# Cell states of a two-layer transformer block finished batch by batch beside the next batch's cells

## What is computed

```python
x = x + tanh(g_xattn[1]) * L1_xattn(layernorm(x), ctx, ctx)   # cells, 16 heads
x = x + tanh(g_ffn[1]) * L1_ffn(layernorm(x))
# in L1_xattn, for each batch and head:
C = (q @ k.T / sqrt(16)) * D            # D = exp(gates), lower triangle
h = (C / (max(|C.sum(-1)|, exp(-m)) + eps)) @ v
h = (h - h.mean(-1)) * rsqrt(h.var(-1) + eps) * ln_scale      # per head
# in L1_ffn, for each token:
inter = silu(q_act(x) @ q_w(w_gate).T) * (q_act(x) @ q_w(w_up).T)
y = q_act(inter) @ q_w(w_down).T        # q_act: blocks of 32, shared exponent, 3 fraction bits
```

## Time and profile before

| what | us |
|---|---|
| median of 3 runs (494.81 to 496.61) | 495.32 |
| the profiled execution, its own time | 496.37 |
| its span, first to last instruction | 494.6 |
| DVE busy in the span | 349.6 |
| PE busy, PE weight load busy | 381.1, 258.7 |
| ACT busy, POOL busy | 189.1, 152.8 |

### The profile page before, as it was taken

The page is one execution under the profiler, slowest core; times in us unless marked ns, Lnnn a source line. Parts: engine busy times, 40 slices in busy tenths (PEclk is TensorE's granted clock), DMA queues, the critical chain, the costliest instruction groups (busy, mean ns, idle before and its releaser), DMA issues.

```text
span 494.6 us, 6936 instructions
## 1 busy us (share of the span) xinstructions
PE 381.1 (77%) x2330; PEld 258.7 (52%) x2330; DVE 349.6 (71%) x857; ACT 189.1 (38%) x331; POOL 152.8 (31%) x147
## 2 busy tenths in 40 slices
PE   7899787799997697959767887979577478660745
PEld 3566454545556585848545555657353156440323
DVE  4586259257633989887976657577995976789895
ACT  4456424323313122603343545444004577640331
POOL 4029300028425445546325223233212020030240
PEclk9999997579998989979995999999697759966695
DMA  8900000003402203302986930907000670000001
GB/s 280 254 12 0 9 1 1 1 1 107 129 0 65 85 12 122 104 20 88 201 187 89 164 104 0 141 31 107 2 0 0 106 129 1 2 0 1 23 20 45
DMA packets 33714, 32.69 MB, mean 66 GB/s; under 512 B 3876, under 2 KB 32784, under 8 KB 33680
## 3 DMA queue, kind: packets, MB, share of 16 engines
q1 hardware_dynamic: 31088, 28.99, 26.4%
q0 software_dynamic: 992, 1.68, 1.2%
q10 hardware_dynamic: 1600, 1.57, 1.0%
HBM read 28.04 MB, written 4.19 MB: 65 GB/s over the span
## 4 chain that ended last, share of the span: by engine, by line
PE 49%; DVE 24%; issue 12%; ACT 6%; POOL 3%; DMA 3%; SPq 1%; DVEq 0%; ACTq 0%; POOLq 0%
PE bank L869 14%; PE bank L895 6%; PE bank L781 5%; PE bank L797 3%; PE bank L754 3%; PE bank L1005 2%; PE bank L969 2%; DVE mxraw L1610 2%; DVE mam L1452 2%; DVE tok L1262 2%; PE bank L765 1%; PE bank L917 1%; PE bank L954 1%; DVE probs L1537 1%; DMA qrep<-part_dram 1%
## 5 line engine op out<-in xcount | busy, mean ns | idle before, releaser
L895 PE MATMUL bank<-wexp,wT 128*128 128x256 f32 x192 | 53.9, 406 | 7.7 <-DVE x L1444 7.6
L869 PE MATMUL bank<-tok_r,probs_r 128*128 128x512 f32 x104 | 48.0, 462 | 11.6 <-DVE wT L1433 7.0
L1322 DVE TENSOR_SCALAR probs<-probs,hi 128x512 f32<-128x512 f32 x64 | 34.6, 592 | 28.8 <-ACT probs L1077 28.7
L663 POOL TENSOR_TENSOR wexp_r<-wexp,probs_r 128x1024 fp32r<-128x1024 f32 x13 | 31.2, 2403 | 60.3 <-ACT probs_r L1088 60.3
L1127 ACT ACTIVATE silu_sb<-bank 128x512 f32<-128x512 f32 x32 | 19.1, 597 | 77.1 <-PE bank L869 77.1
L1077 ACT ACTIVATE probs<-bank 128x1024 f32<-128x1024 f32 x32 | 32.2, 1025 | 41.1 <-PE bank L781 41.1
L591 POOL TENSOR_TENSOR mx_grid<-parts,bl 128x1024 bf16<-128x1024 fp8e4 x9 | 17.2, 1910 | 96.0 <-DVE parts L1613 96.0
L895 PEld LDWEIGHTS bank<-wexp,wT 128*128 128x128 f32 x192 | 37.1, 203 | 15.3 <-issue 10.5
L1537 DVE SCALAR_TENSOR_TENSOR probs<-bank,dexp 128x384 f32<-128x384 f32 x48 | 26.4, 554 | 24.0 <-PE bank L955 17.7
L869 PE MATMUL bank<-tok_r,wexp_r 128*128 128x512 f32 x104 | 42.7, 411 | 0.0
L781 PE MATMUL bank<-qrep,krep 32*128 32x256 f32 x256 | 35.8, 410 | 1.8 <-issue 1.0
(11 more groups left out here) (261 smaller groups left out, 895.9 us busy)
## 6 DMA issues: line engine op xcount, KB each, us to landing
wexp<-in_L_ffn_W SPq DMA_DIRECT2D x28, 256.0 KB, 4.1
krep<-part_dram SPq DMA_DIRECT2D x32, 128.0 KB, 6.6
qrep<-part_dram SPq DMA_DIRECT2D x32, 128.0 KB, 4.6
wexp<-in_L_ffn_Wg SPq DMA_DIRECT2D x14, 256.0 KB, 4.6
part_dram<-parts POOLq DMA_DIRECT2D x4, 384.0 KB, 3.0
part_dram<-parts SPq DMA_DIRECT2D x4, 384.0 KB, 3.3
x<-in_x ACTq DMA_DIRECT2D x2, 512.0 KB, 7.2
ctx<-in_ctx SPq DMA_DIRECT2D x2, 512.0 KB, 7.0
```

What stands on the lines that cost most here:

```text
L663: gp.tensor_tensor(low, raw, w_high[k % 2].bitcast(F32), ALU.subtract).then_inc(s["w_low_ready"], 1)
L869: mm = pe.matmul(bank[:, bk, :], lhs, rhs, start=(kk == 0 and q == 0), stop=(kk == KC - 1 and q == len(terms) - 1))
L895: mm = pe.matmul(bank[:, 2 + pair, D * t:D * t + D], hid[k % 2][m][:, col:col + P], wexp[:, k % WR, 2, m, :], start=(m == 0), stop=(m == 1))
L1322: ins = v.tensor_scalar(w, w, hi[:, 2 * b + kc:2 * b + kc + 1], EM50, ALU.min, ALU.max)
```

## The change

The cell groups run batch by batch: group g is now batch g//2 with heads g%2. So batch 0 is complete after group 1, batch 1 after group 3, batch 2 after group 5, batch 3 after group 7. The finish works on one batch, 2 tiles, 128x512, and there are four of them: batch 0's beside group 3, batch 1's in experts 14 and 15, batch 2's beside group 7, batch 3's behind the last group. GpSimd scales in place in tok and waits for the square in place of the centring. The quantiser of tok works on a batch too (512 columns, items 0, 1, 5 and 8 of now 12); the quantiser of tile 2 stands between scores 33 and 34, that of batch 2 behind score 63; q_turn of tile 1 stands in group 6. krep units 2 and 3 are loaded at groups 2 and 3. quantise(0) stands behind accumulate 31, not before accumulate 30. The functions of DVE, ACT, TensorE and GpSimd take the sizes from q_wide and ln_tiles; where the diff below leaves them out, nothing else changes in them.

```diff
-    def cells(g, first=0):
+    def cells(g, first=0, more=()):
...
-            units.append(u)
+            units.append(u + (more[j] if j < len(more) else []))
...
-    def finish(n):
-        return st("cell_in", n) + st("cell_mid", n) + st("cell_out", n) + st("ln_in", 6 + n) + st("ln_out", 6 + n)
+    def finish(b):
+
+        return [st("cell_in", b), st("cell_mid", b), st("cell_out", b), st("ln_in", 6 + b), st("ln_out", 6 + b)]
+
+    def beside_cells(b, last=[]):
+        f = finish(b)
+        return [f[0], [], f[1], [], f[2], [], f[3], f[4] + last]
 
     plan += expert(8, 5) + weave(expert(9, 6), prepare(0)[:2] + [[]] + prepare(0)[2:4]) + weave(expert(10, 7)[:6], prepare(0)[4:]) + expert(10, 7)[6:8] + st("turn_gates", 0)
-    plan += weave(expert(10, 7)[8:] + flat([expert(k, k - 3) for k in range(11, 14)]), flat([cells(g) for g in range(4)]) + cells_end(3))
-    plan += weave(expert(14, 11) + expert(15, 12), finish(0))
-    plan += st("out", 30, 31) + st("quantise", 0) + st("accumulate", 30, 31)
-
-
-
-    line = [(1, 0), (2, 1), (3, 2), (4, None), (5, 3), (6, 4), (7, 5), (8, 6), (9, 7)]
+    plan += weave(expert(10, 7)[8:] + flat([expert(k, k - 3) for k in range(11, 14)]),
+                  flat([cells(g, 0, beside_cells(0) if g == 3 else ()) for g in range(4)]) + cells_end(3))
+    plan += weave(expert(14, 11) + expert(15, 12), flat(finish(1)))
+    plan += st("out", 30, 31) + st("accumulate", 30, 31) + st("quantise", 0)
+
+
+    line = [(2, 0), (3, 1), (4, 2), (5, None), (6, 3), (7, 4), (8, None), (9, 5), (10, 6), (11, 7)]
...
-    plan += st("q_turn", 0) + ready[:2] + flat(stage_d(0)[:3]) + ready[2:] + flat(stage_d(0)[3:]) + st("turn_gates", 1)
+    plan += ready[:2] + st("q_turn", 0) + st("quantise", 1) + flat(stage_d(0)[:3]) + ready[2:] + st("q_turn", 1) + flat(stage_d(0)[3:]) + st("turn_gates", 1)
     plan += flat(stage_d(1) + stage_d(2)[:3])
-    plan += weave(flat([cells(g, 4) for g in range(4, 8)]), [[]] + stage_d(2)[3:]) + flat(cells_end(7))
-    plan += weave(finish(1), stage_d(3)[:3]) + flat(stage_d(3)[3:])
-    plan += flat(flat([stage_d(j) for j in range(4, len(line) + 4)]))
+    early = stage_d(3)
+    plan += flat(cells(4, 4, [[], stage_d(2)[3]])) + flat(cells(5, 4)) + flat(cells(6, 4, [[], early[0] + early[1] + early[2]]))
+    plan += flat(cells(7, 4, beside_cells(2, early[3])))
+    plan += flat(cells_end(7))
+    plan += weave(flat(finish(3)), stage_d(4) + stage_d(5))
+    plan += flat(flat([stage_d(j) for j in range(6, len(line) + 4)]))
...
-        hstat = arows[:, :, :].rearrange("p a t -> p (a t)")[:, 0:6 * NH * 64].rearrange("p (q n h) -> p q n h", q=6, n=NH)
+        hstat = arows[:, :, :].rearrange("p a t -> p (a t)")[:, 0:6 * B * 32].rearrange("p (q b h) -> p q b h", q=6, b=B)
+        hst = lambda q, b: hstat[:, q, b, :]
...
-        NQ = NT + NH
-        q_half = {0: 0, 4: 1}.get
-        q_tile = lambda k: k - 1 if k < 4 else k - 2
+        q_batch = {0: 0, 1: 1, 5: 2, 8: 3}.get
+        q_tile = {2: 0, 3: 1, 4: 2, 6: 3, 7: 4, 9: 5, 10: 6, 11: 7}.get
+        NQ = NT + B
+        q_wide = lambda k: 2 * D if q_tile(k) is None else NI
 
         def q_source(k):
 
-            if q_half(k) is None:
+            if q_tile(k) is not None:
                 return inter[:, q_tile(k) % 2, :]
-            return tok[:, TH * q_half(k):TH * q_half(k) + TH, :].rearrange("p t d -> p (t d)")
+            return tok[:, 2 * q_batch(k):2 * q_batch(k) + 2, :].rearrange("p t d -> p (t d)")
...
+        def cell_group(g):
+
+            return g // 4, g % 2, g // 2, (g // 2 % 2) * S, 2 * (g // 4) + g % 2
...
+        def ln_tiles(k):
+
+            return range(TH * (k % 2), TH * (k % 2) + TH) if k < 6 else range(2 * (k - 6), 2 * (k - 6) + 2)
+
+        def ln_stat(ap, k):
+            return ap[:, k, :] if k < 6 else ap[:, 6 + (k - 6) // 2, 2 * (k % 2):2 * (k % 2) + 2]
...
-                    sp.wait_ge(s["qk_done"], 16 * (u - 1))
+                    sp.wait_ge(s["qk_done"], 8 * (u + 1))
...
-                if g in (1, 3):
+                if g in (2, 3):
                     sp.wait_ge(s["qk_done"], 8 * (g + 1))
-                    u = (g + 3) // 2
-                    stack_load(sp, krep, u % 2, 1, u, K_TERM, s[f"k_stacked{u}"])
+                    stack_load(sp, krep, g % 2, 1, g, K_TERM, s[f"k_stacked{g}"])
...
-                gp.wait_ge(s["h_centred"], n + 1)
-                gp.tensor_tensor(pvs[:, :, :].rearrange("p a (u d) -> p (a u) d", d=D), tok[:, TH * n:TH * n + TH, :],
-                                 lsc[:, :].unsqueeze(1).broadcast_to([P, TH, D]), ALU.mult).then_inc(s["h_scaled"], 1)
+                gp.wait_ge(s["h_squared"], n + 1)
+                h = tok[:, 2 * n:2 * n + 2, :]
+                gp.tensor_tensor(h, h, lsc[:, :].unsqueeze(1).broadcast_to([P, 2, D]), ALU.mult).then_inc(s["h_scaled"], 1)
...
-                pe.wait_ge(s["xqt_copied"], i // TH + 1)
+                pe.wait_ge(s["xqt_copied"], i // 2 + 1)
...
-                act.activation(mt[:, :, :].rearrange("p a t -> p (a t)"), tok[:, TH * n:TH * n + TH, :].rearrange("p t d -> p (t d)"),
-                               ACT.Square).then_inc(s["h_squared"], 1)
+                act.activation(mt[:, n % 2, :], tok[:, 2 * n:2 * n + 2, :].rearrange("p t d -> p (t d)"), ACT.Square).then_inc(s["h_squared"], 1)
...
+            def cell_in(b):
+
+                v.wait_ge(s["h_placed"], 2 * (b + 1))
+                h3 = tok[:, 2 * b:2 * b + 2, :].rearrange("p t (h v) -> p (t h) v", v=HD)
+                seq.add(v.tensor_reduce(hst(0, b), h3, AX.X, ALU.add))
+                seq.wait()
+                seq.add(v.tensor_scalar(hst(1, b), hst(0, b), 1.0 / HD, None, ALU.mult))
+                seq.wait()
+                v.tensor_tensor(h3, h3, hst(1, b).unsqueeze(2).broadcast_to([P, 32, HD]), ALU.subtract).then_inc(s["h_centred"], 1)
+
+            def cell_mid(b):
+                v.wait_ge(s["h_squared"], b + 1)
+                seq.add(v.tensor_reduce(hst(2, b), mt[:, b % 2, :].rearrange("p (h v) -> p h v", v=HD), AX.X, ALU.add))
+                seq.wait()
+                seq.add(v.tensor_scalar(hst(3, b), hst(2, b), 1.0 / HD, CELL_EPS, ALU.mult, ALU.add))
+                inverse_root(hst(4, b), hst(3, b), hst(5, b), hst(0, b))
+
+            def cell_out(b):
+                v.wait_ge(s["h_scaled"], b + 1)
+                seq.wait()
+                h = tok[:, 2 * b:2 * b + 2, :]
+                h3 = h.rearrange("p t (h v) -> p (t h) v", v=HD)
+                seq.add(v.tensor_tensor(h3, h3, hst(4, b).unsqueeze(2).broadcast_to([P, 32, HD]), ALU.mult))
+                seq.wait()
+                seq.add(v.tensor_tensor(x[:, 2 * b:2 * b + 2, :], x[:, 2 * b:2 * b + 2, :], h, ALU.add))
```

More of the change, by code:

```diff
@@ L934, in cell_exponent @@
                 g, j = w // 8, w % 8
-                n, c, b, _ = group(g)
+                n, c, b, _, _ = cell_group(g)
                 bk = cell_bank(w)[0]
@@ L986, in q_turn @@
                     pe.wait_ge(s["q_ready"], k + 1)
-                n = q_half(k)
-                if n is not None:
-                    bk, reader, count = 6, "xqt_copied", n + 1
+                b = q_batch(k)
+                if b is not None:
+                    bk, reader, count = 6, "xqt_copied", b + 1
                 else:
@@ L992, in q_turn @@
                 claim(bk, reader, count)
-                for q in range(8):
-                    place = 4 * (q % 2) + q // 2 if n is not None else q
+                for q in range(q_wide(k) // P):
+                    place = 2 * (q % 2) + q // 2 if b is not None else q
                     m = pe.transpose(bank[:, bk, 64 * place:64 * place + 64].bitcast(BF16),
@@ L1244, in ln_in @@
                     v.wait_ge(s["x2_acc"], TH * (NE + 1) * (n + 1))
[L1245 to L1246 removed]
+                tiles = ln_tiles(k)
+                for i in tiles:
                     m = seq.add(v.bn_stats(st[:, i, :], x[:, i, :]))
                 seq.wait(m)
[L1249 removed]
+                for i in tiles:
                     m = seq.add(v.bn_aggr(mv[:, i, :], st[:, i, :]))
                 seq.wait(m)
[L1252 to L1253 removed]
+                seq.add(v.tensor_scalar(ln_stat(ve, k), mv[:, tiles.start:tiles.stop, 1], LN_EPS, None, ALU.add))
+                inverse_root(ln_stat(ri, k), ln_stat(ve, k), ru[:, 0, 0:len(tiles)], ru[:, 1, 0:len(tiles)])
             def ln_out(k):
```

72 lines of the change are left out of this document (25 added, 47 removed).

## The result

The changed kernel takes 502.52 us in the median of 4 runs (501.03 to 506.7), the kernel before 495.4: ratio 1.0151, interval 1.0116 to 1.0186. Run again beside other kernels it stood at 1.0129 (1.0091 to 1.0166). So it is slower by 6.4 to 7.5 us, where the prediction's sum was 3.8; the time lies in the range, the sign is right, the forecast size is half of the measured one. The profiled execution took 503.18 us (span 501.3).

The account below looks back on a forecast made before the run. DVE time was taken to bound the kernel, above all the finish alone after the last group. 3.8 - 1.6 - 0.4 + 3.0 + 0.7 + 7.0 - 8.7 = +3.8 us gave median 499.1, range 491.5 to 503.

Parts of the forecast that it names:

- the second unit: Second qrep unit, now needed at cell 8 instead of 16: about nothing, at most 2 us.
- the tail: From score 63's end to the run's end: 54.55 us in place of 63.3, a gain of 8.7.
- group 4: Quantiser of tile 2, 3.85 us, now between scores 33 and 34: cost 3.0 us, bounds 2.0 and 4.0.
- group 3: Batch 0's finish beside group 3's cells, partly in DVE gaps: cost 3.8 us, bounds 1.5 and 4.7.
- the price: Splitting finish and quantiser: half a finish takes 9.05 us of DVE; two halves add 4.3, two half quantisers 1.0.
- group 7: Most of batch 2's finish, 8.35 us, beside group 7's cells: cost 7.0 us, bounds 6.1 and 8.2.
- group 6: Turn and copy of tile 1 beside group 6: cost 0.7 us, as DVE's gap there ends on TensorE.
- the block by GpSimd: Last experts: small DVE instructions wait for GpSimd passes, losing 2.5 of 4.1 us saved on the path to accumulate 26.
- groups 4 and 5: The group 4 term: cost 3.0 us, with TensorE at a mean 0.77 of its clock in this stretch.
- finish in the experts: Half-size finish in the last two experts: gain 1.6 us, bounds 0.5 and 4.1; cell_out and ln_in give nothing.
- between the experts and group 4: Half quantiser behind accumulate 31, gate_up 0 about 0.4 us earlier: gain 0.4, bounds 0 and 1.5.
- The first rival: Expert 14 loses the whole 4.1 us, TensorE doesn't pause before out 28 and keeps 2.4 GHz: -3.4, 491.9; chance 0.17.

## Why the prediction was right in kind and half in size

The mechanism came out as it was told: splitting costs DVE work, the pieces don't fit the holes, and the shorter tail doesn't pay for it. What failed is the size of four terms of the sum. The largest miss is the second unit of the queries' stacks, put at "about nothing" and measured at 1.9 us; then the tail, whose gain of 8.7 was 7.3, group 4 with 4.2 in place of 3.0, and group 3 with 4.6 in place of 3.8. The prediction's bounds held the second unit ("at most 2") and group 3 (4.7), and just missed group 4 (4.0).

By its own steps. Measured costs are differences of means over the profiles of the study that have the piece (seven to ten) and those that have before's in its place (five or six), since single steps scatter by up to 3 us where TensorE's clock or the loads come in.

- **Right: the price.** Half a finish was put at 9.05 of work, 10.25 with waits; measured 10.44 to 10.55. DVE's added work was put at 8 to 10, measured 10.3, just above.
- **Right: group 7**, +7.0, measured 6.7 (normalise 5 to the end of score 63, 9.2 to 15.9); group 6, +0.7, measured 0.5.
- **Right: the block by GpSimd**, also in its number: the path to accumulate 26 was put at 1.6 and not 4.1 shorter, measured 1.9 (16.6 to 14.7). Up to the finish's residual add it is 2.4, as the half-size cell_out, put at nothing, gives 0.5.
- **Mis-sized: the second unit**, "about nothing, at most 2": the stretch up to normalise 0 is 1.9 longer in the mean, and 1.2 to 2.2 in six profiles is the wait itself. The step took cell 8's time and the loads' from the trace of before, where by the median landing of 4.6 about 1 us lay between the last load and the cell; here the eight loads were issued by 279.81, not 277.38, and TensorE was free for cell 8 at 281.80 (285.22 less 3.42), 1.1 ahead of the earlier trace rows. No run that takes the wait away saves time clear of noise, so its worth in the total is argued from the traces.
- **Mis-sized: the tail**, 54.55, measured 56.07 in the changed kernel's first profile: 4.71 to the normaliser, 1.37 for it, 10.45 for finish(3), 31.23 up to the last pass of the last quantiser, 8.31. The 1.0 in the fourth term is the step: 0.8 of it is the 0.99 at 473.99, a wait for GpSimd in the half quantiser that now stands in the line. In the means the gain is 7.3 (63.1 to 55.8), not 8.7.
- **Mis-sized: groups 4 and 5**, +3.0, measured 4.2 (11.48 to 15.64). The 12.7 of before's trace was the slowest of six; the step took its granted clock of 0.77 as given, and in four of the six it was 0.88 to 1.00 and the groups took 11.0 to 11.1.
- **Mis-sized: group 3**, +3.8, measured 4.6 (24.8 to 29.4), in the bounds. The failing step is "cell_in (1.63) falls into the 2.74 gap before 321.67, nothing" and the 1.35 of cover for ln_in. DVE in the changed kernel:

```profile
324.43 0.56 DVE L1556 SCALAR_TENSOR_TENSOR probs<-bank,dexp 128x384 f32<-128x384 f32 x1 [1.96 <-PE bank L975]
...
337.82 0.90 DVE L1241 TENSOR_SCALAR ri<-ve 128x2 int32<-128x2 int32 x1
...
343.89 0.17 DVE L1568 SCALAR_TENSOR_TENSOR rsum<-bank,geT 128x16 f32<-128x16 f32 x1 [1.94 <-PE bank L826]
```

The gaps of 2.74 and 3.47 shrank to 1.96 and 1.94 only. The likely reason is that a piece in front of a gap delays the scores and what TensorE starts behind them, so that most of the gap returns; no run separates it. The 0.90 (otherwise 0.17) is a wait for GpSimd's weight quantiser, which stood in the bound of 4.7 but not in the sum.
- **Right in size: between the experts and group 4**, -0.4, measured -0.9 from the finish to gate math 1 (29.1 to 28.2) and -0.3 from there to score 32. It scatters by 3.7 us between executions of the changed order (26.5 to 30.2), mostly with the clock: finish to last accumulate is 8.8 where out 28 ran at 2.4 GHz and 11.0 to 11.3 where it ran at 1.2. The first rival had 2.9 for this clock, and its condition (no pause before out 28) never came true.

The misses are 1.9 (second unit) + 1.4 (tail) + 1.2 (groups 4 and 5) + 0.8 (group 3), less 0.8 (finish in the experts), 0.5 and 0.3 (between the experts and group 4), 0.3 (group 7) and 0.2 (group 6): 3.2 us. With the 3.8 of the sum that makes 7.0, between the measured 6.4 and 7.5. The misses on the cheap side were luck: without them the forecast would have been 2.1 us further off.
